# A routed transformer block: the order of work around the first expert tiles, re-sequenced on all five engines

## The reference

```python
q = ctx @ Wq.T + bq ; k = ctx @ Wk.T + bk
s = (q @ k.T) * H**-0.5 * layernorm(x)          # 512 x 512 for each sequence
x = x + tanh(g_xattn) * softmax(where(mask, -inf, s))
xn = layernorm(x)
w = sigmoid(xn @ Wg.T)                          # 8 experts, the 2 best of w + bias, normalised
out = x + tanh(g_ffn) * sum_e w_e * ((silu(xn @ W1_e.T) * (xn @ W3_e.T)) @ W2_e.T)
```

## Time and profile before

| | us |
|---|---|
| median of 3 runs | 326.88 |
| lowest, highest | 326.1, 329.94 |
| the profiled execution, its time | 325.86 |
| its span | 323.9 |
| PE, POOL, DVE, ACT busy | 279.9, 196.5, 191.4, 127.3 |
| start of the first `hidden` matmul | 116.56 |

### The profile page before, as it was taken

How to read it: one execution, slowest core, us unless ns; L and a number is a source line. 1 busy time by engine, 2 the same in 40 slices (tenths; PEclk the granted TensorE clock), 3 DMA queues, 4 the chain that set the end, 5 groups by cost and what they waited for, 6 DMA issues and landing times.

```text
span 323.9 us, 5197 instructions
## 1 busy us (share of the span) xinstructions
PE 279.9 (86%) x1316; PEld 203.7 (63%) x1316; DVE 191.4 (59%) x505; ACT 127.3 (39%) x239; POOL 196.5 (61%) x208
## 2 busy tenths in 40 slices
PE   3699799487997696988999996999999999999980
PEld 1145364253354584866888775888888888888860
DVE  2698777899598977598345425444535445454530
ACT  2678569133566652222233222333332332333220
POOL 5188897618777777557776448465646445653313
PEclk9979989655599679999999999999999999999997
DMA  7999898783353361546464657666767556766435
GB/s 230 317 397 328 270 329 301 255 301 138 127 170 133 92 192 34 100 69 101 93 121 76 97 99 112 111 117 110 143 95 124 108 83 115 134 126 97 46 54 65
DMA packets 27026, 48.69 MB, mean 150 GB/s; under 512 B 9524, under 2 KB 10296, under 8 KB 25976
## 3 DMA queue, kind: packets, MB, share of 16 engines
q0 software_dynamic: 9760, 20.49, 36.1%
q1 hardware_dynamic: 14408, 15.04, 14.5%
q10 hardware_dynamic: 2832, 12.85, 11.7%
HBM read 28.51 MB, written 19.85 MB: 149 GB/s over the span
## 4 chain that ended last, share of the span: by engine, by line
DMA 45%; issue 19%; POOL 11%; PE 10%; DVE 9%; ACT 3%; POOLq 2%; SPq 1%; ACTq 0%; DVEq 0%
DMA out<-rows,slot 30%; DMA out<-rows 10%; POOL out L460 4%; POOL rows L441 4%; PE bank L902 2%; DMA rows<-in_x 2%; POOL slot_table L428 2%; POOLq L452 2%; DVE w_lo L841 1%; DMA w_hi<-in_ctx_t 1%; DVE rows L698 1%; DMA rows<-xn_rows,slot 1%; DVE w_hi L675 1%; PE bank L909 1%; PE bank L981 1%
## 5 line engine op out<-in xcount | busy, mean ns | idle before, releaser
L460 POOL DMA_INDIRECT out<-rows,slot x39 | 62.3, 1598 | 65.4 <-DMA out<-rows,slot 42.1
L993 PE MATMUL bank<-w_hi,xt_hi 128*128 x156 | 64.7, 414 | 0.0
L994 PE MATMUL bank<-w_lo,xt_hi 128*128 x156 | 61.1, 392 | 0.0
L995 PE MATMUL bank<-w_hi,xt_lo 128*128 x156 | 61.0, 391 | 0.0
L820 DVE TENSOR_TENSOR xt_lo<-bank,xt_hi 128x512 fp32r<-128x512 f32 x39 | 26.9, 690 | 50.7 <-ACT xt_hi L584 50.7
L592 ACT ACTIVATE rows<-bank 128x256 f32<-128x256 f32 x39 | 15.0, 384 | 88.1 <-PE bank L995 88.1
L441 POOL DMA_INDIRECT rows<-xn_rows,slot x39 | 39.2, 1005 | 16.2 <-issue 10.2
L605 ACT ACTIVATE rows<-bank,slot 128x512 f32<-128x512 f32 x39 | 26.8, 687 | 50.0 <-PE bank L1022 39.0
L428 POOL DMA_INDIRECT slot_table<-entry,slot_index x32 | 33.1, 1034 | 17.8 <-DVE slot_index L783 9.0
L826 DVE SCALAR_TENSOR_TENSOR rows<-rows,bank 128x256 f32<-128x256 f32 x39 | 16.4, 420 | 38.7 <-ACT rows L592 38.5
L1020 PE MATMUL bank<-w_hi,gt_hi 128*128 x78 | 30.9, 396 | 4.8 <-DVE gt_lo L837 4.8
(11 more groups left out here) (131 smaller groups left out, 454.6 us busy)
## 6 DMA issues: line engine op xcount, KB each, us to landing
w_lo<-in_w ACTq DMA_DIRECT2D x8, 1024.0 KB, 7.6
xn_rows<-w_hi SPq DMA_DIRECT2D x17, 256.0 KB, 6.8
rows<-in_x SPq DMA_DIRECT2D x16, 256.0 KB, 4.3
out<-rows SPq DMA_DIRECT2D x16, 256.0 KB, 3.9
w_lo<-in_w ACTq DMA_DIRECT2D x8, 512.0 KB, 4.5
w_hi<-in_ctx_t SPq DMA_DIRECT2D x4, 256.0 KB, 5.3
slot<-slot_table SPq DMA_DIRECT2D x39, 1.0 KB, 2.2
rows<-xn_rows,slot POOLq DMA_INDIRECT x39, 4.3
```

The lines of the kernel that those rows point to most:

```text
L460: pool.indirect_dma_start(out=out[0:SPARE + P * READY[segment(i)], :], out_offset=bass.IndirectOffsetOnAxis(ap=slot[:, i, 0:1].bitcast(U32 ...
L993: pe.matmul(ps_h[i % 2][:], xt_hi[:, i % 2, k, :], hi, start=(k == 0), stop=False)
L994: pe.matmul(ps_h[i % 2][:], xt_hi[:, i % 2, k, :], lo, start=False, stop=False)
L995: mm = pe.matmul(ps_h[i % 2][:], xt_lo[:, i % 2, k, :], hi, start=False, stop=(k == KC - 1))
```

## The change

The same instructions in other places. (1) `store_x1` goes from SP's queue to ACT's, right behind `squares`. (2) Weight loads are issued up to two steps later, and more units are split in steps 8 to 14. (3) The projection of the next sequence takes the place of the filler matmuls (`spin`) in its step on PE, and comes after the exponentials of the following step on ACT. (4) The first group's slots are made and entered one step earlier; its tile slots are loaded two steps earlier, 3 of them ahead of the store of normalised tile 12. (5) Gathers 0 and 1 come in step 14 instead of after step 15; `gathered_hi(0)` stands ahead of the last exponentials on ACT, `gathered_lo(0)` ahead of the last residual on DVE. (6) The transposes of token tiles 14 and 15 and the logits of 13 to 15 move in among the first expert tiles on PE. (7) Weights and slots of the second group move from before the first expert tile to expert tiles 0 and 1, its slot entries on POOL behind gather 4, its list to tile 2; the third group moves one tile later. (8) Buffers: the scores of tiles 14 and 15 use the row buffer of x tile 12, their normalised rows and transposes overwrite their own x row, other PSUM banks take `hidden`, `output` and positions.

```diff
     PIECE = W13 // 2
-    SPLITS = (1, 1, 2, 2, 1, 2, 1, 2, 1, 1, 1, 2, 1, 1, 2, 1)
-    LO_BY_POOL = (0, 1, 2, 4, 6, 7, 9, 10)
...
-    SCATTERS = {9: (0, 0, 3), 10: (0, 3, 6), 11: (0, 6, 10), 12: (0, 10, 14)}
...
+    SPLITS = (1, 1, 1, 1, 1, 2, 1, 1, 2, 2, 2, 2, 1, 2, 2, 1)
+    LO_BY_POOL = (0, 1, 2, 3, 4, 6, 7, 9)
...
+    SCATTERS = {8: (0, 0, 3), 9: (0, 3, 7), 10: (0, 7, 11), 11: (0, 11, 14)}
...
     SPINS = 5
...
 attn_neg = early(10, 2).bitcast(BF16).rearrange("p (t s) -> p t s", t=NT)
-prob = early(14, 1)
+q_sb = early(12, 1)
+k_sb = early(13, 1)
+xt_sb = early(14, 1)
+xn_odd = early(15, 1)
 bqk_sb = sb("bqk_sb", [P, 2])
...
+def prob(tile):
+    return x_row(TILES - 4) if tile >= TILES - 2 else prob_sb
+
 def normed_row(tile):
-    if tile == TILES - 1:
-        return x_row(TILES - 3)
-    return early(15, 1) if tile % 2 == 0 else early(13, 1)
+    if tile >= TILES - 2:
+        return x_row(tile)
+    return xn_even if tile % 2 == 0 else xn_odd
 def normed_columns(tile):
-    row = x_row(TILES - 2) if tile == TILES - 1 else early(12, 1)
+    row = x_row(tile) if tile >= TILES - 2 else xt_sb
     return row.rearrange("p (k s) -> p k s", k=KC)
...
-    def store_x1(tile):
-        sp.wait_ge(s_x1, tile + 1)
-        sp.dma_start(out[SPARE + tile * P:SPARE + (tile + 1) * P, :], x_row(tile)).then_inc(s_x1_out[tile % XR], 16)
-
     def store_xn(tile):
         sp.wait_ge(s_xn, tile + 1)
+        if tile >= TILES - 2:
+            sp.wait_ge(s_xn_out[tile % 2], 16 * (tile // 2))
         sp.dma_start(xn_rows[SPARE + tile * P:SPARE + (tile + 1) * P, :], normed_row(tile)).then_inc(s_xn_out[tile % 2], 16)
...
             reuse_x(step - 2)
-        if step == TILES - 1:
+        if step == TILES - 3:
             listed(0)
-            for i in range(4):
+            for i in range(3):
+                load_slots(i)
+        elif step == TILES - 2:
+            for i in range(3, FIRST[1]):
                 load_slots(i)
-        if 1 <= step <= TILES:
-            store_x1(step - 1)
         if step % NT == 3 and step // NT + 2 < B:
             load_ctx(step // NT + 2)
-        if step == TILES - 1:
-            for i in range(4, FIRST[1]):
-                load_slots(i)
     for k in (1, 2):
...
             pool.wait_ge(s_x, i - XG + 1)
+        elif i == XG - 1:
+            pool.wait_ge(s_exp, TILES)
         else:
...
             enter_slots(*SCATTERS[step])
-    gather(0)
-    gather(1)
+        if step == TILES - 2:
+            gather(0)
+            gather(1)
+    gather(2)
     row_scales(TILES)
     normed(TILES - 1)
-    gather(2)
     gather(3)
-    enter_slots(1, 0, 6)
     for i in range(LIST):
...
+    def store_x1(tile):
+        act.wait_ge(s_x1, tile + 1)
+        act.dma_start(out[SPARE + tile * P:SPARE + (tile + 1) * P, :], x_row(tile)).then_inc(s_x1_out[tile % XR], 16)
+
     def transposed(tile):
...
         if unit == 2 * E + 3:
-            act.wait_ge(s_proj, 2 * B)
-            act.wait_ge(s_scores, TILES)
+            act.wait_ge(s_exp, TILES - 2)
+            act.wait_ge(s_xpose, TILES - 3)
+            act.wait_ge(s_xn_out[0], 16 * (TILES // 2 - 1))
         if unit == 2 * E + 4:
+            act.wait_ge(s_proj, 2 * B)
             act.wait_ge(s_neg, TILES)
         if unit == 2 * E + 6:
-            act.wait_ge(s_logits, TILES - 1)
+            act.wait_ge(s_scores, TILES)
+        if unit == 2 * E + 7:
+            act.wait_ge(s_logits, TILES - 2)
             act.wait_ge(s_xpose, TILES - 2)
             act.wait_ge(s_xn_out[1], 16 * (TILES // 2 - 1))
-        if unit == 2 * E + 7:
-            act.wait_ge(s_exp, TILES)
-            act.wait_ge(s_xpose, TILES - 1)
-            act.wait_ge(s_xn_out[0], 16 * (TILES // 2))
         act.copy(high(unit), raw(unit)).then_inc(s_hi, 1)
...
         else:
-            row_done(TILES - 3 + i)
-            if i == 0:
-                act.wait_ge(s_xpose, TILES)
-                act.wait_ge(s_xn_out[1], 16 * (TILES // 2))
-            else:
-                act.wait_ge(s_logits, TILES)
+            act.wait_ge(s_logits, TILES - 1 + i)
         act.activation(y[:, i % 2, :], ps_o[i % 2][:], ACT.Copy, scale=slot[:, i, 1:2].bitcast(F32)).then_inc(s_y, 1)
...
     for step in range(TILES):
+        if step == TILES - 1:
+            gathered_hi(0)
         exponentials(step)
+        if step % NT == 3 and step // NT + 1 < B:
+            project(step // NT + 1)
+        if step == TILES - 1:
+            gathered_hi(1)
         if step >= 2:
             transposed(step - 2)
-        for unit in units_in(step)[0:2]:
-            if unit != 2 * E + 4:
-                split_hi(unit)
+        for unit in units_in(step):
+            split_hi(unit)
         if step == END[0] + 1:
...
         squares(step)
-        if step == TILES - 2:
-            split_hi(2 * E + 4)
-        if step % NT == 2 and step // NT + 1 < B:
-            project(step // NT + 1)
+        store_x1(step)
         for n in LOADS.get(step, ()):
             load_weights(n)
-    transposed(TILES - 2)
-    split_hi(UNITS - 2)
-    gathered_hi(0)
-    transposed(TILES - 1)
-    gathered_hi(1)
-    split_hi(UNITS - 1)
     for i in range(LIST):
         hidden_tanh(i)
+        if i == 0:
+            split_hi(UNITS - 1)
+            transposed(TILES - 2)
+        elif i == 1:
+            transposed(TILES - 1)
         if i > 0:
...
         dve.wait_ge(s_scores, tile + 1)
-        dve.scalar_tensor_tensor(out=prob, in0=x_row(tile), scalar=mv1[:, t, 0:1],
+        if tile == TILES - 2:
+            dve.wait_ge(s_xn, TILES - 3)
+            dve.wait_ge(s_x1_out[(TILES - 4) % XR], 16 * ((TILES - 4) // XR + 1))
+        dve.scalar_tensor_tensor(out=prob(tile), in0=x_row(tile), scalar=mv1[:, t, 0:1],
                                  in1=ps_s[tile % 2][:], op0=ALU.subtract, op1=ALU.mult).then_inc(s_z, 1)
...
             first_stats(step + 3)
+        if step == TILES - 1:
+            gathered_lo(0)
         residual(step)
...
             router_weights(0)
-        elif step == END[0] + 2:
             router_slots(0)
+        elif step == END[0] + 2:
             list_tiles(0)
-    router_ranks(1)
-    router_weights(1)
-    gathered_lo(0)
-    router_slots(1)
     gathered_lo(1)
-    for unit in range(2 * E + 5, UNITS):
+    for unit in units_in(TILES - 1):
         split_lo(unit)
+    router_ranks(1)
     for i in range(LIST):
         gate_rows(i)
+        if i == 0:
+            split_lo(UNITS - 1)
         if i + 2 < LIST:
...
         if i == 0:
-            list_tiles(1)
+            router_weights(1)
+        elif i == 1:
+            router_slots(1)
         elif i == 2:
-            router_ranks(2)
+            list_tiles(1)
         elif i == 3:
+            router_ranks(2)
+        elif i == 4:
             router_weights(2)
             router_slots(2)
-        elif i == 4:
+        elif i == 5:
             list_tiles(2)
...
-    def spin(projected):
-        pe.wait_ge(s_qk, 2 * projected)
+    def spin(step):
+        if step > END[0] + 1:
+            pe.wait_ge(s_slots, 2)
+            pe.wait_ge(s_ls, 1)
         for _ in range(SPINS):
-            pe.matmul(ps_q[:], ident_bf[:], attn_neg[:, 0, :], start=True, stop=True)
+            pe.matmul(ps_early[:], ident_bf[:], attn_neg[:, 0, :], start=True, stop=True)
...
             pe.wait_ge(s_gated, i - 1)
-        else:
-            pe.wait_ge(s_sq, TILES - 1 + i)
+        elif i == 1:
+            pe.wait_ge(s_sq, TILES - 1)
         for k in range(KC):
...
         else:
-            pe.wait_ge(s_slots, 4)
+            pe.wait_ge(s_zmax, TILES)
         for c in range(FC):
...
         else:
+            pe.wait_ge(s_sq, TILES)
             pe.wait_ge(s_lo_dve, sum(lo_by_dve(unit) for unit in range(UNITS)))
...
     pe.wait_ge(s_wg_in, 16)
-    projected = 1
     for step in range(TILES):
...
             masks(step + 1)
-        if step == END[0] + 2:
-            positions(0)
-        if step < TILES - 2:
-            spin(projected)
-        if step >= 2:
-            logits(step - 2)
-        if step >= 1:
-            transpose(step - 1)
         if step % NT == 2 and step // NT + 1 < B:
             project(step // NT + 1)
-            projected += 1
-    logits(TILES - 2)
+        elif step < TILES - 2:
+            spin(step)
+        if 2 <= step < TILES - 1:
+            logits(step - 2)
+        if 1 <= step < TILES - 1:
+            transpose(step - 1)
+        if step == END[0] + 1:
+            positions(0)
     gathered(0)
-    positions(1)
-    transpose(TILES - 1)
     gathered(1)
...
         if i == 0:
-            logits(TILES - 1)
+            logits(TILES - 3)
+            transpose(TILES - 2)
             gathered(2)
...
             gate_transpose(0)
+            logits(TILES - 2)
+            transpose(TILES - 1)
             gathered(3)
...
             gate_transpose(1)
+            logits(TILES - 1)
+            positions(1)
         else:
...
                 gathered(i + 2)
```

(2 more changed lines are left out.)

54 lines of the change are left out of this document (27 added, 27 removed).

## The result

The changed kernel takes 339.0 us (median of 4 runs, 337.01 to 342.97), against 327.01 (326.1 to 329.94) for the kernel before on the same chip: ratio 1.033, 95% interval 1.023 to 1.043, slower. The profiled execution took 339.99, its span 338.0. The prediction was 331.0, at most 336.

The account below looks back on a forecast made before the run. The prediction took the chain of POOL's adds, starting with add 0, to bound the kernel, then PE alone. 325.86 plus 3.5 for a later add 0 and 1.3 for one more entry gave 330.7, stated as 331.0; range 323 to 336.

Parts of the forecast that it names:

- What matters is when add 0 starts: Expert tiles: the chain of POOL's adds into the output sets the pace; add 0 was forecast 3.5 us later, at 135.2.
- Hidden 0 itself is not on that path: Start of expert tiles: hidden 0, forecast 10 us earlier at 106.6, does not decide when add 0 starts.
- Rivals A and D: A: hidden 0's 10 us gain reaches the end, 316 (8%). D: the late POOL and unit 19 don't bite, 325.8 (15%).
- both late things: First phase, tiles 8 to 15: POOL late through group 1's entries, 2.0 us; unit 19 waiting for a store, 2.9 us.
- the first entry, predicted at 123.3: POOL's first slot entry of group 2, after DVE's slots: forecast at 123.3, 5.4 us later than 117.86.
- Eight free steps ... That is 47.7 for tile 8: Early first phase: steps of 4.01 us plus a low part and two projections bring tile 8's scores 4.7 us earlier.
- rival C: Early steps gain nothing because DMA engines limit loads and stores: tile 8 stays at 52.4, end 335; chance 10%.
- Tile 8 to 15, 48.0 + 2.0 + 2.9 = 52.9: Later first phase: 48.0 us if nothing else is late, 2.0 for late POOL, 2.9 for unit 19's wait.
- 2.0 in sum, between 0 and 4: Later first phase: PE's transposes wait because POOL, busy with group 1's entries, normalises tiles 10 and 11 late; 2.0 us.
- From tile 15 to the first entry, 22.7: From tile 15's scores at 100.6, through last store, gather 3, output 0 and group 2's slots, to the entry at 123.3.
- The 1.3 for one more entry ahead of gather 15: Adds on POOL: turn 10 has two entries where it had one, paid ahead of gather 15; 1.3 us.
- Rival B: Start of expert tiles: PE's clock falls to half, hidden 0 and 1 take 3.6 us more, end 334; chance 22%.

Follow-up runs that it names:

- e14: Changed kernel with the unit splits, POOL low parts, weight loads and group 1 entries of the kernel before: ratio 1.013 to the kernel before.
- e15: e14 with PE's filler spins also in the projection steps: ratio 1.006 to the kernel before.
- e16: e15 with group 2's slots ahead of the expert tiles, last exponentials first, group 2's list and group 3 in old turns: ratio 0.984 to the kernel before.
- e6: Kernel before with six unused powers on POOL ahead of add 0: ratio 1.010 to the kernel before.
- e7: Kernel before with the twelve matmuls of hidden 0 done twice: ratio 1.004 to the kernel before.
- e18: e16 with the copy and low part of gathered tile 0 again ahead of the last exponentials and residual: ratio 0.981 to the kernel before.
- e4: Changed kernel with the high part of unit 19 one step later (14, not 13): ratio 1.029 to the kernel before.
- e12: Changed kernel with slots early, last exponentials first, unit 19 later, late lists back, and spins added in the projection steps: ratio 1.009 to the kernel before.
- e13: Changed kernel with POOL taking the low part of unit 8 in place of unit 9: 334.5 us, one run.
- e10: Changed kernel with PE spins added in the three projection steps: ratio 1.024 to the kernel before.
- e17: e16 with the projections back behind the squares, spins in every step: ratio 0.985 to the kernel before.
- e5: Kernel before with only the x1 stores moved to ACT's queue: ratio 0.991 to the kernel before.
- e11: e5 with the projection's two ACT passes behind the next exponentials: ratio 0.991 to the kernel before.
- e3: Changed kernel with the last exponentials and residual again ahead of gathered tile 0's copy and low part: ratio 1.036 to the kernel before.

## Why the prediction was wrong

**The cost by parts.** Taken back one after the other, the parts give 1.033 for the changed kernel, 1.013 with the old tables (e14), 1.006 with the spins too (e15), and 0.984 with the slots of group 2, the last exponentials and the late parts in their old places (e16). The last step joins several parts, and which of them has how much of it isn't told apart by time.

**What held.** "What matters is when add 0 starts", "Hidden 0 itself is not on that path": 15.2 at add 0 were 14.1 at the end, and e6, e7 and e18 agree. "Moving the slots into the expert tiles costs": the first entry waited 7.80 for them, from tile 15 to it 25.6 (predicted 22.7, before 14.0). First entry to add 0: 11.6, predicted 11.9. Hidden 16 behind add 11: 9.8, as predicted. Rivals A and D are out: hidden 0 didn't count, and both late things cost time.

**What failed: the first entry, predicted at 123.3, came at 135.3.** The 12.0 are three steps of the sum.

- *"Eight free steps ... That is 47.7 for tile 8"*: 51.6, 3.9 too late. Two terms stood at nothing. One is PE's clock: I priced the projection's two ACT passes at 1.3 and not the spins that PE lost in the same step, and in this profile tile 5 waited 2.98 for PE at 1.2 GHz. The other is waits for x: a free step has none, and tile 4 waited 2.32. At the full clock tile 8 still came at 49.4 to 50.2 in e4, e12 and e13, 2 us behind the forecast, with 3.9 to 4.8 of waits for x. e10 alone meets the 47.7, and in part by luck, since 1.92 of waiting for x is in it. So rival C (52.4) was wrong on the size and right that waits for loads remain.
- *Tile 8 to 15, 48.0 + 2.0 + 2.9 = 52.9*: 58.1, 5.2 too long. By the terms of the sum: from tile 8 to 10 it is 3.5 too long, of which 2.1 are one operation of DVE that POOL's low part kept out, which no step of mine had, and 1.4 a wait for the router's tanh. From tile 10 to 12 the sum is right (12.0, predicted 12.1). From 12 to 15 it is 1.8 too long: unit 19 cost 3.35 for 2.9, the rest, by subtraction, is POOL ("2.0 in sum, between 0 and 4", near 3.3). The prediction had the mechanism of both, not their size and reach. Of unit 19's wait the slot loads ahead of the store on SP made 4.0 (99.5 to 103.5), where I had 1.3, and POOL was ready with tile 12 at 99.5 where I had 92.8 (my own terms add up to 92.5). POOL became the chain of the whole stretch, and the old tables alone take 6.8 off (e14).
- *From tile 15 to the first entry, 22.7*: 25.6. The store of the last x1 row was to land in 2.3; issued at 118.13, it let POOL go on at 123.45, 5.3 later, so gather 3 stood 14.7 behind tile 15 and not 11.9. A median of three stores from a quiet stretch was the wrong row: the changed kernel's page has 3.7 for these stores.

**Errors on the other side.** Add 0 to the end: 193.1, predicted 195.5. The 1.3 for one more entry ahead of gather 15 didn't come, since add 10 stood 7.1 behind add 9, as before (7.4); and add 3 followed add 2 by 3.2 in place of 5.8, its rows being long ready. Sum: 12.0 - 0.3 - 2.4 = 9.3, from 330.7 to 339.99.

**Rival B.** PE did start the expert tiles at 1.2 GHz (the first six matmuls of hidden 0 took 0.57 to 0.79, the other six 0.39 or 0.40), and hidden 0 came 7.7 behind tile 15 where I had 6.0. But in e16 and e18 hidden 0 starts with the same 0.79 and 0.63, and they are the fastest kernels beside e17. It isn't what made the change slow.

**The rule on DMA queues.** The Trainium skill (DMA: Bandwidth & Descriptors, "Issuing engines are not separate DMA queues") says that issuing DMAs from several engines only saves the sequencer's time for it. No run here shows what the DMA engines share. By that rule alone part (1) gains nothing; moving the stores alone gained 0.9% in e5 (0.987 to 0.996). The likely reason is the order of SP's queue, in which stores and loads stood behind each other's waits, but the waits for x don't bear it out alone: 7.7 before and 2.1 in e5, 6.2 in e6 and 5.6 in e11.

## What to carry to other kernels

Find the event from which the end follows at a fixed distance (here add 0: 192.8 to 194.7 from it to the end in 12 of the 20 kernels, though the starts of add 0 differ by 20; 191.2 to 198.7 in the others), and price each part of a change by what it does to that event alone. A part that takes filler matmuls away, or puts a second engine's work into the same step, must be priced for the clock and for the engine that stands next in line, not only for the instructions moved. One profile of a kernel is one draw: the same code up to tile 8 had it anywhere from 49.4 to 51.6. A move ahead of a wait is free only if what it waits for is there: the same move of gathered tile 0 cost 1.4 at add 0 in one kernel and 0.4 in another, in which gather 0 was issued ahead of the last scores.

## What the runs showed of the hardware

**POOL and DVE keep each other out.** While POOL subtracted a low part (72.21, 2.35 long) a DVE comparison of 1 x 6 elements (L816), both inputs in SBUF, took 2.29 and ended with it; with that low part elsewhere it took at most 0.173 (e13). The other way round: a power on POOL took 1.75 at 89.30 while DVE made two low parts (89.25, 2.35), and 0.69 to 0.76 in eleven of the thirteen of its shape; the other long one, 1.82 at 96.66, stood beside a low part on DVE too (96.68). The Trainium skill (SBUF — State Buffer, "SBUF: two separate sides") calls the pair of ports that the two engines share an exclusive lock, held for the whole instruction, also for a DVE operation with two SBUF inputs against a GpSimd one that reads SBUF; by that rule, the trace agrees. On the page this doesn't show as waiting, but as busy time of an operation that is too long for its size.

**The clock behind a step without fillers.** Without them, behind the projection, the clock from 24 to 36 us was 0.66, 0.66 and 0.73 in the changed kernel, e14 and e3, and 1.00 in e4 and e13. PE had waited 1.96 for the projection's copies in the three, 0.42 and 1.26 in the two. With them at the same place (e10, e12, e15, e16, e18) it was 1.00 each time, and PE had waited 0.2 to 0.9. Fillers are no warrant: the kernel before has them in every one of these steps and had 0.86 from 36 to 48 us, e6 with the same steps 0.72.
